# A decoder layer on one core: a piece behind the weighting in four quads, and two pieces of the row maximum copied by ScalarE and merged by GpSimd

## The chip, the cores and the metric

One core of one Trainium2 chip runs the whole kernel in one launch. The metric is the device time in microseconds; lower is better. TensorE does the matmuls, VectorE (DVE) and ScalarE (ACT) read what it leaves in PSUM, GpSimd (POOL) works on SBUF, SyncE (SP) issues most transfers.

## The reference, cut to what matters

The layer is causal self-attention, then attention over a context, then a mixture of experts, each followed by a layer norm. The change is in the self-attention, with S = 2048 rows, D = 256, H = 16 heads of 16 columns:

```python
scores = jnp.einsum('bhqd,bhkd->bhqk', q, k) / jnp.sqrt(jnp.float32(Dh))
causal = jnp.tril(jnp.ones((S, S), dtype=bool))
scores = jnp.where(causal[None, None], scores, jnp.float32(-jnp.inf))
attn = jax.nn.softmax(scores, axis=-1)
out = jnp.einsum('bhqk,bhkd->bhqd', attn, v)
```

The softmax is computed with the maximum of each row of scores taken off, and that maximum is found before the head's exponentials are.

## The kernel before

`project` forms q, k, v and the context's matrices, `attend` does the 16 heads, `finish` the rest. The change touches `attend`, and one place in `project`.

**A head** is cut into ten quads (QUADS), each of 512 queries by four tiles of 128 keys; quads 0, 2, 5 and 9 are on the diagonal and smaller. In each quad s, TensorE's queue holds in this order: the first half of the scores (`scores_half(h, s, 0)`, L747, two matmuls, one in each half of the array's rows, the row groups 0 and 1; on the diagonal also the small matmuls of L756 that hide later keys), the entries of place 0, the second half of the scores, the entries of place 1, the weighing of the quad two before (`weigh`, L774, fp32, eight matmul records, all 128 rows), and the entries of place 2. `scores_half` of the next quad waits until ScalarE has taken the exponential of the same half (L709, 1024 or 640 columns, written to `probs`). ScalarE also copies the accumulator `acc` when a block of queries ends (L714, behind the exponentials of quads 1, 2, 4 and 7), and the folded sums (L721, quad 4). A block's first weighing waits for the copy of the block before.

**The maximum of the rows** is found a head or two ahead. For it the scores are formed once more with queries on the partitions, in 35 pieces of up to 512 columns (`form_piece`, L154, and L161 for the diagonal), each in a bank of a ring of three (`ring`, NRING = 3). A piece uses one row group: `given` adds up the columns that each group has had since the last half of scores, and the group with the smaller sum takes the next piece (the first on a tie). Its VectorE reduction (`reduce_piece`, L172) writes a column or more of `partial` and frees the bank; TensorE waits for the bank's last user before it forms entry e + 3. Three other entries run through the ring: "F" folds the sums of the head before (copied by ScalarE), "M" turns `neg_max`, and "T" turns the folded sums, which VectorE normalises (L836, L838).

The table PLACES says which entries stand in the three places of each quad: "w" a whole piece of 512, "d" one on the diagonal, "n" one of 384, "p" and "q" two of 256 and four of 128 together. The pieces of quads 0 to 5 are for the next head, those of quads 6 to 9 (EARLY_QUADS) for the one after it. So the last piece for the next head stands in quad 5; behind it VectorE reduces `partial` to `neg_max` (L850) and waits for that before it goes on, since `partial` is written again. In quad 8 the maximum goes through the ring, VectorE writes `max_row` (L855), and SyncE sends it to the rows of `qstack` that the next head's scores wait for. The first head's pieces, and the early ones of the second, are formed in `project` (`pieces_behind`), 51 in all.

**GpSimd** meanwhile turns the experts' weights to two f16 halves, a sixteenth a head: multiply (L684), cast (L687), subtract (L689), each on 2304 columns. SyncE loads and stores them at the head's end, behind the maximum's rows and the loads of a later head's stacks.

Of the kernel before, what the change touches and what calls it, by code (L numbers as in the profile page):

```python
# [8 lines left out]
H = 16  # L9
# [4 lines left out]
P = 128  # L14
# [40 lines left out]
def cut_pieces():  # L55
# [11 lines left out]
    for quarters, found in share.items():  # L67
# [26 lines left out]
(FOLD_AT,) = [s for s, places in enumerate(PLACES) if "F" in "".join(places)]  # L94


def kind_of(n):
    if len(PIECES[n]) > 1:
        return {2: "p", 4: "q"}[len(PIECES[n])]
    ((t, c, w),) = PIECES[n]  # L100
    return "n" if w < QB else "d" if c + w == (t + 1) * P else "w"
# [16 lines left out]
def ring_of(h):  # L118

    def entry(s, x):  # L120
        kind, ahead = OTHERS[x] if x in OTHERS else ("piece", 2 if s in EARLY_QUADS else 1)
        return (kind, h + ahead, 0 if x in OTHERS else x)
# [8 lines left out]
TAKEN = [sum(x[0] != "fold" for x in ENTRIES[0:e + 1]) for e in range(len(ENTRIES))]  # L131
FOLDS = [sum(x[0] == "fold" for x in ENTRIES[0:e + 1]) for e in range(len(ENTRIES))]
# [33 lines left out]
def reduce_piece(nc, X, ALU, bank, partial, n):  # L166

    found = partial[:].rearrange("p t b -> p (t b)")
# [31 lines left out]
def decoder_layer(nc, x, xT, ctx_n, ctxT, wq, wk, wv, wo, b_qk, bv, bo, lm, w_all, gT, out):  # L200
# [15 lines left out]
    with whole:  # L216
# [10 lines left out]
        with ExitStack() as two:  # L227
            attn = two.enter_context(nc.sbuf_tensor("attn", [P, NT, DH + D], f32))
            with ExitStack() as three:
# [6 lines left out]
                partial = three.enter_context(nc.sbuf_tensor("partial", [P, NT, NQ], f32))  # L236
# [22 lines left out]
def project(nc, f32, f16, ALU, ACT, x, xT, ctx_n, ctxT, wq, wk, wv, wo, b_qk, bv, bo, lm, gT,  # L259
# [7 lines left out]
    with es:  # L267
# [183 lines left out]
        def _(dve):  # L451
# [7 lines left out]
            def take_pieces(count):  # L459
                nonlocal taken  # L460
                for _ in range(count):
# [4 lines left out]
                    if m == NPIECE:  # L466
                        dve.wait_ge(first_max_found, 1)
                    reduce_piece(nc, X, ALU, piece_ps[m % NRING], partial, FIRST_PIECES[m]).then_inc(piece_done, 1)
                    taken += 1
                    if taken == NPIECE:  # L470
                        dve.wait_ge(piece_done, NPIECE)
                        nc.vector.tensor_reduce(out=neg_max[:], in_=partial[:], axis=X, op=ALU.max, negate=True).then_inc(first_max_found, 1)
# [108 lines left out]
def attend(nc, f32, f16, bf16, ALU, ACT, X, q_split, k_split, w_all, w_split_d, res, bo_rows, ident32, attn, values,  # L581
# [6 lines left out]
    with es:  # L588
# [8 lines left out]
        folded = sb("folded", [P, QB], f32)  # L597
        inv = sb("inv", [P, 2, TPQ, NQ, 1], f32)
# [7 lines left out]
        ring_ready, ring_done, fold_copied = sem("ring_ready"), sem("ring_done"), sem("fold_copied")  # L606
        max_found = sem("max_found")
# [6 lines left out]
        def wait_taken(engine, e):  # L614

            if ENTRIES[e][0] == "fold":
                engine.wait_ge(fold_copied, FOLDS[e])
# [31 lines left out]

        block = es.enter_context(nc.Block())  # L650
# [1170 lines left out]
```

## Time and profile before

| | us |
|---|---|
| median of 3 runs | 841.28 |
| lowest and highest | 839.92, 846.05 |
| the profiled execution | 842.19 |
| its span, from the first to the last instruction | 840.5 |
| mean granted TensorE clock | 0.981 |

A span is what the traced instructions cover; an execution's time holds a little more. Times in the rows below are microseconds from the span's start. The `attend` part runs from 88.3 to about 470 us.

### The profile page before, as it was taken

How to read it: one execution, taken by the hardware profiler on the slowest of the kernel's cores; microseconds unless marked ns; L12 is line 12 of the kernel's file. 1: busy time of each engine (PE TensorE's matmuls, PEld its weight loads, DVE VectorE, ACT ScalarE, POOL GpSimd, SP SyncE). 2: the span in 40 equal slices, each digit the busy share in tenths (PEclk: the TensorE clock that was granted, in tenths of full speed). 3: DMA queues.
4: the chain of work that ended last, by engine and by line, in shares of the span. 5: the costliest groups of instructions: out<-in, count | busy, mean ns of one | idle time of the engine just before them, and what ended most of it. 6: DMA issues, size and time to landing. Idle time of an engine off the chain costs nothing. (4 is left out here: it accounts for less than half of the span.)

```text
span 840.5 us, 19596 instructions
## 1 busy us (share of the span) xinstructions
PE 788.1 (94%) x7434; PEld 494.6 (59%) x7435; DVE 555.8 (66%) x1072; ACT 513.0 (61%) x756; POOL 304.3 (36%) x226
## 2 busy tenths in 40 slices
PE   5899999999999999999998798889999999999994
PEld 1367334434444434444433586778888888877883
DVE  4575699999999999999980397973333333322395
ACT  4441587778877877788879487354444444343543
POOL 5040595554333455553640012142333333301121
PEclk9999799999999999999999998999999999999997
DMA  9683343333444433334332498462222222221362
GB/s 299 124 215 152 113 150 104 101 127 133 146 151 152 152 118 108 113 132 138 113 115 114 191 411 202 147 209 60 76 76 75 75 76 75 78 59 51 98 198 76
DMA packets 68362, 111.47 MB, mean 133 GB/s; under 512 B 39485, under 2 KB 49918, under 8 KB 63934
## 3 DMA queue, kind: packets, MB, share of 16 engines
q1 hardware_dynamic: 63134, 93.36, 35.4%
q0 software_dynamic: 4816, 16.65, 6.0%
q10 hardware_dynamic: 336, 0.40, 0.4%
q8 instruction: 54, 0.88, 0.4%
q14 instruction: 22, 0.18, 0.1%
HBM read 66.60 MB, written 32.37 MB: 118 GB/s over the span
## 5 line engine op out<-in xcount | busy, mean ns | idle before, releaser
L172 DVE TENSOR_REDUCE partial<-ring 128x1 f32<-128x512 f32 (+3 forms) x509 | 308.6, 667 | 28.4 <-PE ring L154 18.4
L709 ACT ACTIVATE probs<-scores 128x1024 f32<-128x1024 f32 (+1 forms) x320 | 271.5, 902 | 65.5 <-PE scores L756 31.8
L1284 ACT ACTIVATE hid<-turned 128x512 f32<-128x512 f32 (+1 forms) x112 | 65.6, 586 | 160.6 <-PE turned L1445 130.6
L774 PE MATMUL acc<-probs,values 128*32 128x512 f32 (+2 forms) x1472 | 156.4, 495 | 0.5 <-ACT acc_sb L714 0.3
L1470 PE MATMUL ops<-weights,work 128*128 (+1 forms) x1320 | 148.9, 273 | 2.6 <-issue 2.0
L154 PE MATMUL ring<-kstack,qstack 48*128 48x512 f16 (+1 forms) x580 | 147.8, 354 | 2.5 <-DVE partial L172 0.2
L1445 PE MATMUL turned<-mats,weights 128*128 128x256 f16 (+1 forms) x1344 | 144.2, 262 | 2.4 <-DMA mats<-attn 1.6
L1470 PEld LDWEIGHTS ops<-weights,work 128*128 128x128 f16 x1320 | 128.4, 98 | 18.8 <-issue 3.8
L1685 DVE TENSOR_TENSOR work<-hid,work 128x512 f16<-128x512 f32 (+1 forms) x112 | 76.8, 690 | 94.8 <-ACT work L1289 94.8
L684 POOL TENSOR_TENSOR a_w_in<-a_w_in,w_scale 128x2304 f32<-128x2304 f32 x16 | 64.4, 4026 | 204.2 <-DMA a_w_in<-w_all 204.2
L1445 PEld LDWEIGHTS turned<-mats,weights 128*128 (+1 forms) x1344 | 122.5, 98 | 21.0 <-issue 3.7
L747 PE MATMUL scores<-qstack,kstack 49*128 49x512 f16 (+3 forms) x640 | 127.8, 353 | 4.5 <-ACT probs L709 3.2
L1209 POOL DMA_INDIRECT by_token<-attn,dest_u x39 | 38.7, 992 | 143.5 <-DVE attn L1694 137.7
L154 PEld LDWEIGHTS ring<-kstack,qstack 48*128 48x128 f16 x580 | 44.3, 94 | 77.5 <-DVE partial L172 63.4
L747 PEld LDWEIGHTS scores<-qstack,kstack 49*128 49x128 f16 x640 | 39.0, 94 | 80.6 <-ACT probs L709 58.0
L689 POOL TENSOR_TENSOR a_w_out<-a_w_in,a_w_out 128x2304 f16<-128x2304 f32 x16 | 73.1, 4569 | 1.3
L1289 ACT ACTIVATE work<-hid 128x512 f16<-128x512 f32 (+1 forms) x112 | 69.7, 622 | 4.6
L774 PEld LDWEIGHTS acc<-probs,values 128*32 128x32 f32 x1472 | 43.5, 108 | 36.6 <-issue 25.6
L1694 DVE COPY attn<-ops 128x512 f32<-128x512 f32 (+1 forms) x20 | 13.6, 678 | 68.7 <-PE ops L1470 68.7
L161 PE MATMUL ring<-hide_keys,ident 64*128 64x128 bf16 x460 | 51.3, 203 | 0.0
L161 PEld LDWEIGHTS ring<-hide_keys,ident 64*128 64x128 bf16 x460 | 41.3, 95 | 15.6 <-issue 0.7
L1201 POOL DMA_INDIRECT attn<-rows_d,token_u x39 | 38.5, 988 | 30.0 <-issue 10.7
(203 smaller groups left out, 741.0 us busy)
## 6 DMA issues: line engine op xcount, KB each, us to landing
a_w_in<-w_all SPq DMA_DIRECT2D x16, 1152.0 KB, 8.9
w_split_d<-a_w_out SPq DMA_DIRECT2D x16, 1152.0 KB, 5.6
weights<-w_split_d SPq DMA_DIRECT2D x6, 2048.0 KB, 19.8
weights<-w_split_d POOLq DMA_DIRECT2D x3, 2048.0 KB, 11.8
qstack<-q_split SPq DMA_DIRECT2D x72, 64.0 KB, 2.7
kstack<-k_split SPq DMA_DIRECT2D x72, 64.0 KB, 2.7
weights<-by_token SPq DMA_DIRECT2D x8, 512.0 KB, 7.6
attn<-xT SPq DMA_DIRECT2D x4, 512.0 KB, 7.5
```

The source lines that it names most:

```text
L154: mm = nc.tensor.matmul(bank[:, at:at + w], qstack[rows, slot, t * P:(t + 1) * P], kstack[rows, slot, c:c + w], start=True, stop=not diagonal)
L161: mm = nc.tensor.matmul(bank[:, at - P + a:at - P + b], ident16[rows, copy], hide_keys[rows, copy, a:b], start=False, stop=part == 1)
L172: return nc.vector.tensor_reduce(out=found[:, places[0]:places[-1] + 1:step], in_=bank[:, 0:WIDTH[n]].rearrange("p (k w) -> p k w", k=len( ...
L689: nc.gpsimd.tensor_tensor(w_out[:, h % 2, 1], w_in[:, h % 2], w_out[:, h % 2, 0], ALU.subtract).then_inc(w_lo, 1)
L709: nc.scalar.activation(probs[:, quad % NPROBS, at:at + w], scores[half][:, first:first + w], ACT.Exp, scale=QK_SCALE).then_inc(exp_done, 1)
L747: mm = nc.tensor.matmul(scores[half][:, at:at + w], kstack[used, slot, kt * P:(kt + 1) * P], qstack[used, slot, (qb + 1) * QB - w:(qb + 1) ...
L774: mm = nc.tensor.matmul(acc[VW * group:VW * (group + 1), first_query:first_query + w], values[:, h, k0 + j], probs[:, quad % NPROBS, at:at ...
L1284: nc.scalar.activation(h32, hps[b].rearrange("p (j n) -> p j n", n=TW)[:, :, 0:w], ACT.Silu, scale=1.0 / WSCALE).then_inc(silu_done, 1)
L1289: nc.scalar.activation(hid[:, parity, 0, b * HB:(b + 1) * HB, 0:w], h32, ACT.Copy).then_inc(hid_hi, 1)
L1445: mm = nc.tensor.matmul(place.rearrange("p (g n) -> p g n", n=P), weights[:, a, bass.ds(at + (k * HID + (b * HB + j) * P), P)], turned_row ...
L1470: mm = nc.tensor.matmul(bank[:, i], hid[:, parity, a, j, i * P:(i + 1) * P], weights[:, c, bass.ds(at + (WE // 2 + j * D), D)], start=(m = ...
L1685: nc.vector.tensor_tensor(hid[:, parity, 1, chunks, 0:w], hid32[:, b % 2].rearrange("p (j n) -> p j n", n=TW)[:, :, 0:w], hid[:, parity, 0 ...
```

## The change

- PLACES: in quads 0, 2, 5 and 6 one "w" now stands in place 2, behind the weighing; it comes out of place 0 of the quad after (quads 1, 3, 6, 7). One "w" of quad 0 and one of quad 2 become "c".
- The two "c" are the first two column blocks of the last row tile (t = 15). TensorE forms them as before. Then ScalarE copies the bank to `copies` in SBUF (behind the exponentials of quads 0 and 2) and frees the bank; VectorE doesn't reduce them.
- GpSimd merges the two copies by a maximum, written as a + clamp(b - a), in twelve dependent operations: three on 512 columns, then three on each of 256, 128 and 64, which fold the halves of the copy onto one another. It does so between the cast and the subtraction of the weights.
- VectorE takes the maximum of what is left (64 columns to 2) and then reduces `partial` to `neg_max`; both stand ahead of the last entry of quad 7 (MAX_BEHIND), no longer behind the last piece in quad 5. It waits for GpSimd there.
- `partial` has two sets, one for even and one for odd heads.
- In `project` 50 pieces are formed and not 51, since the early quads hold one fewer.

```diff
-PLACES = (("", "wd", ""), ("ww", "w", "nw"), ("", "ww", ""), ("dw", "w", "w"), ("", "ww", "Fwp"),
-          ("", "wn", ""), ("ww", "d", ""), ("ww", "n", "w"), ("qMT", "wd", "nw"), ("", "ww", "wp"))
+PLACES = (("", "cd", "w"), ("w", "w", "nw"), ("", "cw", "w"), ("d", "w", "w"), ("", "ww", "Fwp"),
+          ("", "wn", "w"), ("w", "d", "w"), ("w", "n", "w"), ("qMT", "wd", "nw"), ("", "ww", "wp"))
...
+MAX_BEHIND = 7
+MERGED = 64
...
-        return 2 if n % 4 == 3 else 1 if n == DC * CT - 1 else 0
+        return 2 if n % 4 == 3 else 0
...
-                partial = three.enter_context(nc.sbuf_tensor("partial", [P, NT, NQ], f32))
+                partial = three.enter_context(nc.sbuf_tensor("partial", [P, 2, NT, NQ], f32))
...
+            def merge_copies(g):
+
+                at = (g - 1) * MERGES
+                pool.wait_ge(ring_copied, COPIES[COPIED[g][-1]])
+                w = QB
+                while w >= MERGED:
+                    a, b = (copies[:, 0], copies[:, 1]) if w == QB else (copies[:, 0, 0:w], copies[:, 0, w:2 * w])
+                    if w < QB:
+                        pool.wait_ge(merged, at)
+                    nc.gpsimd.tensor_tensor(above[:, 0:w], b, a, ALU.subtract).then_inc(merged, 1)
+                    pool.wait_ge(merged, at + 1)
+                    nc.gpsimd.tensor_scalar(above[:, 0:w], above[:, 0:w], -NEG, 0.0, ALU.min, ALU.max).then_inc(merged, 1)
+                    pool.wait_ge(merged, at + 2)
+                    nc.gpsimd.tensor_tensor(a, a, above[:, 0:w], ALU.add).then_inc(merged, 1)
+                    at += 3
+                    w //= 2
...
+            def copy_piece(g, i):
+                e = COPIED[g][i]
+                act.wait_ge(ring_ready, e + 1)
+                if i == 0 and g > 1:
+                    act.wait_ge(merged_found, g - 1)
+                nc.scalar.activation(copies[:, i], ring[e % NRING][:], ACT.Copy).then_inc(ring_copied, 1)
...
                     exps(h, s)
+                    if s in COPY_AT and h + 1 < H:
+                        copy_piece(h + 1, COPY_AT.index(s))
...
+                if e in MAX_FOUND_AT:
+                    found = MAX_FOUND_AT[e]
+                    dve.wait_ge(ring_done, TAKEN[LAST_PIECE[found]])
+                    dve.wait_ge(merged, found * MERGES)
+                    nc.vector.tensor_reduce(out=partial[:, found % 2, NT - 1, 0:2], in_=copies[:, 0, 0:MERGED].rearrange("p (k w) -> p k w", k=2),
+                                            axis=X, op=ALU.max).then_inc(merged_found, 1)
+                    dve.wait_ge(merged_found, found)
+                    nc.vector.tensor_reduce(out=neg_max[:], in_=partial[:, found % 2], axis=X, op=ALU.max,
+                                            negate=True).then_inc(max_found, 1)
                 dve.wait_ge(ring_ready, e + 1)
                 if kind == "piece":
-                    reduce_piece(nc, X, ALU, bank, partial, n).then_inc(ring_done, 1)
-                    if e == LAST_PIECE[g]:
-                        dve.wait_ge(ring_done, TAKEN[e])
-                        nc.vector.tensor_reduce(out=neg_max[:], in_=partial[:], axis=X, op=ALU.max,
-                                                negate=True).then_inc(max_found, 1)
-                        dve.wait_ge(max_found, g)
+                    reduce_piece(nc, X, ALU, bank, partial, g, n).then_inc(ring_done, 1)
```

## Rows read from the trace of the kernel before

**Rows 1.** The page, part 1: engine, busy us (share of the span), instructions.
```profile
PE 788.1 (94%) x7434; PEld 494.6 (59%) x7435; DVE 555.8 (66%) x1072; ACT 513.0 (61%) x756; POOL 304.3 (36%) x226
```

**Rows 2.** Busy time in a 25 us stretch of attention; then clock, DMA share, GB/s.
```profile
core 0: us, PE busy (x) PEld busy (x) DVE busy (x) ACT busy (x) POOL busy (x), PEclk, DMA share, GB/s
225.00:250.00 25.00, 24.74 (x264) 10.06 (x262) 23.31 (x42) 20.20 (x27) 11.52 (x4) 1.00 0.38 128
```

**Rows 3.** VectorE's timeline over one head: start, length, instruction, idle before it.
```profile
205.52 0.27 DVE L855 TENSOR_SCALAR max_row<-ring 16x128 f16<-16x128 f32 x1
...
212.88 4.14 DVE L172 TENSOR_REDUCE partial<-ring 128x1 f32<-128x512 f32 x7 [0.31 <-PE ring L154]
217.31 3.84 DVE L172 TENSOR_REDUCE partial<-ring 128x1 f32<-128x512 f32 x6 [0.30 <-PE ring L161]
221.73 2.35 DVE L172 TENSOR_REDUCE partial<-ring 128x1 f32<-128x512 f32 x4 [0.57 <-PE ring L154]
224.11 0.22 DVE L850 TENSOR_REDUCE neg_max<-partial 128x16 f32<-128x64 f32 x1
224.54 4.94 DVE L172 TENSOR_REDUCE partial<-ring 128x1 f32<-128x512 f32 x8 [0.20 <-PE ring L154]
229.39 0.27 DVE L855 TENSOR_SCALAR max_row<-ring 16x128 f16<-16x128 f32 x1
```

**Rows 4.** VectorE's timeline from 226.5 us on.
```profile
226.52 2.95 DVE L172 TENSOR_REDUCE partial<-ring 128x1 f32<-128x512 f32 x5
```

**Rows 5.** TensorE's timeline from 223.8 to 225 us: quad 6.
```profile
223.83 0.39 PE L747 MATMUL scores<-qstack,kstack 49*128 49x512 f16 x2
224.05 0.38 PE L154 MATMUL ring<-kstack,qstack 48*128 48x512 f16 x2
...
224.88 0.64 PE L774 MATMUL acc<-probs,values 128*32 128x512 f32 x4
```

**Rows 6.** TensorE's weight loads over the same head, with what they waited for.
```profile
215.28 0.09 PEld L154 LDWEIGHTS ring<-kstack,qstack 48*128 48x128 f16 x1 [0.32 <-DVE partial L172]
...
219.22 0.10 PEld L747 LDWEIGHTS scores<-qstack,kstack 49*128 49x128 f16 x2 [0.47 <-ACT probs L709]
...
222.25 0.31 PEld L154 LDWEIGHTS ring<-kstack,qstack 48*128 48x128 f16 x2 [0.15 <-ACT folded L721]
...
222.83 0.16 PEld L774 LDWEIGHTS acc<-probs,values 128*32 128x32 f32 x8
```

**Rows 7.** TensorE's timeline from 217.5 to 219.6 us: a lone piece behind a weighing.
```profile
217.64 1.06 PE L774 MATMUL acc<-probs,values 128*32 128x512 f32 x8
218.64 0.39 PE L154 MATMUL ring<-kstack,qstack 48*128 48x512 f16 x1
218.65 0.97 PE L747 MATMUL scores<-qstack,kstack 49*128 49x512 f16 x4
```

**Rows 8.** Groups by line and shape, 130 to 400 us: busy, mean ns, idle before.
```profile
L172 DVE TENSOR_REDUCE partial<-ring 128x1 f32<-128x512 f32 x317 | 202.4, 683 | 17.3 <-PE ring L154 11.9 <-PE ring L161 3.3
```

**Rows 9.** ScalarE's timeline over the same head.
```profile
212.69 1.94 ACT L709 ACTIVATE probs<-scores 128x1024 f32<-128x1024 f32 x2 [0.79 <-PE scores L747]
...
214.99 1.32 ACT L709 ACTIVATE probs<-scores 128x640 f32<-128x640 f32 x2
216.74 0.60 ACT L714 ACTIVATE acc_sb<-acc 128x512 f32<-128x512 f32 x1 [0.43 <-PE acc L774]
217.24 3.99 ACT L709 ACTIVATE probs<-scores 128x1024 f32<-128x1024 f32 x4
```

**Rows 10.** GpSimd's timeline over the same head.
```profile
223.32 4.03 POOL L684 TENSOR_TENSOR a_w_in<-a_w_in,w_scale 128x2304 f32<-128x2304 f32 x1 [12.81 <-DMA a_w_in<-w_all]
227.41 2.10 POOL L687 CAST a_w_out<-a_w_in 128x2304 f16<-128x2304 f32 x1
229.59 4.57 POOL L689 TENSOR_TENSOR a_w_out<-a_w_in,a_w_out 128x2304 f16<-128x2304 f32 x1
```

**Rows 11.** GpSimd's groups by line and shape: its shortest rows with two large inputs.
```profile
L443 POOL TENSOR_TENSOR values<-values,bv_rows 128x256 f32<-128x256 f32 x16 | 11.2, 721 | 29.4 <-ACT values L387 29.4
```

**Rows 12.** GpSimd's timeline in the first head.
```profile
97.94 2.10 POOL L687 CAST a_w_out<-a_w_in 128x2304 f16<-128x2304 f32 x1
```

More of the change, by code:

```diff
@@ L87 @@
 EARLY_QUADS = tuple(range(6, NQUAD))
[L91 to L92 removed]
+PLACES = (("", "cd", "w"), ("w", "w", "nw"), ("", "cw", "w"), ("d", "w", "w"), ("", "ww", "Fwp"),
+          ("", "wn", "w"), ("w", "d", "w"), ("w", "n", "w"), ("qMT", "wd", "nw"), ("", "ww", "wp"))
 OTHERS = {"M": ("max", 1), "F": ("fold", -1), "T": ("turn", -1)}
 (FOLD_AT,) = [s for s, places in enumerate(PLACES) if "F" in "".join(places)]
+COPY_AT = [s for s, places in enumerate(PLACES) if "c" in "".join(places)]
+MAX_BEHIND = 7
+MERGED = 64
+assert len(COPY_AT) == 2
 def kind_of(n):
@@ L100, in kind_of @@
     ((t, c, w),) = PIECES[n]
+    if t == NT - 1 and c // QB < len(COPY_AT):
+        return "c"
     return "n" if w < QB else "d" if c + w == (t + 1) * P else "w"
@@ L120, in entry @@
     def entry(s, x):
-        kind, ahead = OTHERS[x] if x in OTHERS else ("piece", 2 if s in EARLY_QUADS else 1)
+        kind, ahead = OTHERS[x] if x in OTHERS else ("copied" if kind_of(x) == "c" else "piece", 2 if s in EARLY_QUADS else 1)
         return (kind, h + ahead, 0 if x in OTHERS else x)
@@ L130 @@
 ENTRY_AT = {x: e for e, x in enumerate(ENTRIES)}
-TAKEN = [sum(x[0] != "fold" for x in ENTRIES[0:e + 1]) for e in range(len(ENTRIES))]
-FOLDS = [sum(x[0] == "fold" for x in ENTRIES[0:e + 1]) for e in range(len(ENTRIES))]
+BY_ACT = ("fold", "copied")
+TAKEN = [sum(x[0] not in BY_ACT for x in ENTRIES[0:e + 1]) for e in range(len(ENTRIES))]
+COPIES = [sum(x[0] in BY_ACT for x in ENTRIES[0:e + 1]) for e in range(len(ENTRIES))]
+COPIED = {g: [e for e, (kind, of, _) in enumerate(ENTRIES) if (kind, of) == ("copied", g)] for g in range(1, H)}
+MAX_FOUND_AT = {ENTRY_AT[([x for place in RING[g - 1][MAX_BEHIND] for x in place] or [("max", g, 0)])[-1]]: g for g in range(1, H)}
 LAST_PIECE = {g: e for e, (kind, g, _) in enumerate(ENTRIES) if kind == "piece"}
@@ L163, in form_piece, with reduce_piece @@
     return mm
-def reduce_piece(nc, X, ALU, bank, partial, n):
-    found = partial[:].rearrange("p t b -> p (t b)")
+def reduce_piece(nc, X, ALU, bank, partial, g, n):
+    found = partial[:, g % 2].rearrange("p t b -> p (t b)")
     places = [t * NQ + c // QB for t, c, _ in PIECES[n]]
@@ L471, in take_pieces @@
                         dve.wait_ge(piece_done, NPIECE)
-                        nc.vector.tensor_reduce(out=neg_max[:], in_=partial[:], axis=X, op=ALU.max, negate=True).then_inc(first_max_found, 1)
+                        nc.vector.tensor_reduce(out=neg_max[:], in_=partial[:, 0], axis=X, op=ALU.max, negate=True).then_inc(first_max_found, 1)
                     if taken == NPIECE + 2:
@@ L597, in attend @@
         folded = sb("folded", [P, QB], f32)
+        copies = sb("copies", [P, 2, QB], f32)
+        above = sb("above", [P, QB], f32)
         inv = sb("inv", [P, 2, TPQ, NQ, 1], f32)
@@ L720, in copy_folded @@
                     act.wait_ge(ring_ready, ENTRY_AT["turn", h - 1, 0] + 1)
-                nc.scalar.activation(folded[:], ring[e % NRING][:], ACT.Copy).then_inc(fold_copied, 1)
+                nc.scalar.activation(folded[:], ring[e % NRING][:], ACT.Copy).then_inc(ring_copied, 1)
+            def copy_piece(g, i):
[4 more added lines that the diff above has]
+                nc.scalar.activation(copies[:, i], ring[e % NRING][:], ACT.Copy).then_inc(ring_copied, 1)
             for h in range(H):
@@ L800, in through_ring @@
                         wait_taken(pe, e - NRING)
-                    if kind == "piece":
+                    if kind in ("piece", "copied"):
                         group = given.index(min(given))
```

19 lines of the change are left out of this document (10 added, 9 removed).

## The prediction

> **What bounds the kernel now.** The page comes first: TensorE is busy 94% of the span, VectorE 66%, and both are crowded only while attention runs [rows 1]. The table by stretches shows that part alone: in 25 us of attention TensorE is busy 24.74, VectorE 23.31, ScalarE 20.20 and GpSimd 11.52 us [rows 2]. So three engines are near their limits, and the share of busy time can't say which one sets the pace. What does is the order within one head. A head lasts 229.39 - 205.52 = 23.87 us (from one writing of max_row to the next, [rows 3]), and the head I walk through is that one. It has ten quads. In each, TensorE writes scores, forms pieces into the ring of three banks, and weighs (the fp32 matmuls of L774).
>
> The VectorE timeline [rows 3] shows idle time before four groups of reductions (0.31 us at 212.88, 0.30 at 217.31, 0.57 at 221.73, 0.20 at 224.54), each time until TensorE had formed a piece. From 226.52 on there is none up to the maximum at 229.39: five reductions in 2.95 us, then max_row [rows 3, 4]. So VectorE sets the pace only in the last third of the head (quads 7 to 9, and on into quad 0 of the next); in quads 0 to 6 it waits for TensorE. There TensorE runs without a hole: after the weighing at 222.83 scores start at 223.83, two pieces side by side at 224.05, and the next weighing at 224.88, 2.05 us in all [rows 5]. The waits of TensorE's loads in the same head [rows 6] are for VectorE at 215.28, for ScalarE at 219.22 and 222.25. (An idle of weight loads behind a weighing is mostly its own streaming, 1.00 us from 217.64 to 218.64 [rows 7], and is no wait.)
>
> **The change, part by part.**
>
> *Two pieces a head off VectorE.* A reduction of 512 costs 0.68 us alone [rows 8] and about 0.60 from start to start (five in 2.95 us, one of them a shorter one [rows 4]). Two fewer are 1.2 us a head less. But they leave in quads 0 and 2, just ahead of the idle at 212.88 and 217.31 [rows 3], where the next piece isn't formed yet: the saved time becomes longer idle. One small thing is gained: the wait at 215.28 for a bank gets shorter by up to 0.2. I count the removal as 0. The other bound is the whole 1.2 us (the first rival).
>
> *One piece behind the weighting in quads 0, 2, 5 and 6.* Before, quads 1, 3, 6 and 7 form two pieces side by side ahead of the second scores. Now one stands directly behind the weighing, the other alone. This needn't cost TensorE anything. At 218.64 a lone piece (row group 1) starts with the scores of row group 0 (218.65), and the second scores matmul follows in the group that comes free [rows 7]. The next lone piece then goes to group 0 beside it. Reading `given`: in quads 0, 2 and 6 the smaller sum is that of group 1, so the piece pairs so. In quad 5 it is a tie (384 + 384 against 256 + 512), and the index of the minimum is group 0. Then group 0 has one stream of 512 more, and that costs what one takes, 224.05 - 223.83 = 0.22 us [rows 5]. The gain: VectorE gets its first piece behind a weighing 0.22 us sooner. The loss: the second scores matmul comes 0.22 later, and the exponential behind it 0.18 (estimate: it takes the start of the last matmul).
>
> *ScalarE's two copies.* Nearest row: the 512 copy from PSUM, 0.60 us, 0.50 from its start to the next exponential (216.74 to 217.24) [rows 9]. The first copy falls into ScalarE's idle before 212.69, which it fits. The second: ScalarE works without a break from 212.69 to 216.31 and has 0.43 us idle before 216.74 [rows 9]. All this now comes 0.18 later, the copy ends near 216.94 and the accumulator's copy starts near 216.82. That is 0.08 late. But the piece of quad 3 (formed at about 216.8 now) needs the bank that the copy frees at 216.99: TensorE stands 0.18 us, with the second scores and the weighing of quad 3 queued behind it. Of that 0.10 is returned at 219.22, where TensorE waited for an exponential anyway [rows 6], and 0.08 stays. The wait for `folded` at 222.25 doesn't add to it, since the diagonal piece next to it waits for VectorE as long. With the tie's 0.22 TensorE is 0.28 us late (0.07 + 0.21 before rounding) at the weighing in quad 7. Bounds: 0 (all waits swallow it) to 0.45 (the `folded` path passes on its 0.18).
>
> *VectorE's maximum, now at the end of quad 7.* Before, one reduction of 64 columns at 224.11, 0.22 us, half in an idle stretch [rows 3]. After, two in a chain, the second of which waits for the first, ahead of the last piece of quad 7, in the stretch without idle: 0.22 + 0.03 + 0.22, less 0.05 that the next overlaps, 0.42 us. The 0.03 is what lies between the four reductions that ended at 221.73 + 2.35 = 224.08 and the one at 224.11 that waited for them [rows 3]. Bounds 0.35 and 0.60. The maximum's transpose and everything behind it on VectorE wait for that.
>
> *GpSimd's merging.* Twelve dependent operations a head on 512, 256, 128 and 64 columns. Nearest rows: 2304 columns with two inputs 4.03 us (1.75 ns a column), with one input 2.10 (0.91); 256 columns 0.72 us (2.8 ns) [rows 10, 11]. The two-input ones, 2 x 960 columns, give 3.4 us at 1.75 and 5.4 at 2.8, the others 0.9 to 2.7, twelve hand-overs of some 0.07 (227.35 to 227.41 [rows 10]) 0.9 us: 5.2 to 9.0, I take 7.3. The second copy ends at 216.9 and VectorE asks for the result near 228.2 (226.52 + 2.95, less the last two reductions, 1.28 [rows 4]), so 11.3 us hide it. GpSimd has room: 10.8 of 23.87 us busy a head. The store and the next load of the weights queue behind its last subtraction, which ends about 216.9 + 7.3 + 4.6 = 228.8, before SyncE comes to it at the head's end. In the first head merging can begin only when the cast ends, 97.94 + 2.10 = 100.04 [rows 12], later in the head's course than in any other; what its cover lacks there is lost once and not in every head.
> The Trainium skill (GPSIMD Engine Reference, "Elementwise — side-by-side cycle accounting") gives 4497 ns for a two-input operation on 2048 columns, 2.2 ns a column. By it the two-input ones would take 4.2 us instead of 3.4 at the long rows' rate, and the sum for the head would be unchanged. The page's larger price isn't what this case's 4.03 us for 2304 columns shows.
>
> *Partial maxima in two sets.* They drop a wait of VectorE that [rows 3] shows at 224.33 to 224.54, in idle time: 0. One piece fewer in the projection takes one reduction, 0.68 us [rows 8], off its end and adds as much to the first head.
>
> **The sum.** At the end of quad 7 VectorE is late by 0.28 (TensorE's delay) - 0.22 (the piece behind the weighing) + 0.42 (the two reductions) = 0.48 us. From there to quad 0 of the next head the two are bound to each other, so the head is 0.48 longer. There are 13 full heads (the first starts loosely; the last two form few pieces or none ahead): 13 x 0.48 = 6.2 us. The profiled execution took 842.19 us, 840.5 of it the span; 840.5 + 6.2 = 846.7, and 842.19 + 6.2 = 848.4. It lies 0.9 above the median of the runs, 841.28, so the median should be 841.28 + 6.2 = 847.5.
>
> **The rivals.**
> A. VectorE is the bound throughout. For it: 23.31 of 25 us busy. Then the head shortens by 1.2 - 0.42 = 0.78 us, over 14 heads 10.9: 830.4. Against it: four idles a head, two of them where the pieces are taken off. It decides if those idles disappear.
> B. The delays are swallowed: TensorE 0 late, and 0.42 - 0.22 = 0.20, with the bank's wait at 215.28 gained back: 0 to 0.2 a head, 841 to 844; I say 842. For it: three waits of TensorE a head that may give way.
> C. All delays add: 0.45 - 0.22 + 0.60 = 0.83 a head, 13 x 0.83 = 10.8: 852.
> D. Merging is too long. At over 11.3 us VectorE stands in front of it in every head; at 13 us that is 1.7 us x 15 = 25: 867. Against it: even the rate of the shortest row gives 9.0.
>
> **How the numbers follow.** My forecast 0.50 (843.5 to 851 by itself), A 0.09, B 0.20, C 0.15, D 0.06. What a measurement of this kernel can tell from no change is about 1%, 8.4 us: below 832.9, above 849.7. Faster: A, 0.08. Slower: C, D and three tenths of the forecast, 0.35. Within: 0.57. The range leaves out A, D and edges: 838 to 855, which reaches from B to C.
>
> **What would show it.** In the profile after: a head of about 24.35 us; VectorE idle before the first piece of quads 1 and 3 longer than 0.3 us; ScalarE's copies near 0.6 us; TensorE waiting for ScalarE's second copy for some 0.2 us; the weighings around the tie 0.2 further apart; both small reductions near 0.22 us in a stretch without idle; GpSimd's twelve operations done in 5 to 9 us before VectorE asks. I am wrong if the idles behind the weighings vanish (A), if no weighing comes later than before up to quad 7 (B), or if VectorE waits for GpSimd (D).

## The result and the profile after

| | before | after |
|---|---|---|
| median, us (lowest to highest) | 841.24 (839.92 to 846.05) | 849.91 (846.77 to 850.99) |
| the profiled execution, its span | 842.19, 840.5 | 850.39, 848.6 |
| mean granted TensorE clock | 0.981 | 0.978 |
| one head, max_row to max_row | 23.87 | 24.39 |

The changed kernel takes 1.0089 times the time before, with an interval from 1.0070 to 1.0109. The span is 8.1 us longer, and 8.0 of it lies ahead of the end of attention: from the span's start to the first matmul behind attention it is 472.24 us before and 480.25 after. The page, part 1, of the kernel after (engine, busy us, share, instructions), and the same 25 us of attention as in [rows 2]:

```profile
PE 790.6 (93%) x7434; PEld 499.3 (59%) x7435; DVE 544.5 (64%) x1057; ACT 526.5 (62%) x786; POOL 409.1 (48%) x406
```
```profile
225.00:250.00 25.00, 24.19 (x266) 10.43 (x260) 22.01 (x40) 20.56 (x29) 18.26 (x16) 1.00 0.40 128
```

VectorE fell from 23.31 to 22.01 us busy in the stretch and TensorE from 24.74 to 24.19, at a granted clock of 1.00 (2.4 GHz) in both. TensorE has the same work in each head, but a head takes longer, so that less of it falls into 25 us. More is waited for. One head on VectorE after, to be held against [rows 3] (start, length, instruction, idle before it and what ended it):

```profile
257.27 0.27 DVE L900 TENSOR_SCALAR max_row<-ring 16x128 f16<-16x128 f32 x1
...
264.41 3.58 DVE L182 TENSOR_REDUCE partial<-ring 128x1 f32<-128x512 f32 x6 [0.62 <-PE ring L164]
268.61 1.98 DVE L182 TENSOR_REDUCE partial<-ring 128x1 f32<-128x512 f32 x3 [0.62 <-PE ring L164]
271.05 1.99 DVE L182 TENSOR_REDUCE partial<-ring 128x1 f32<-128x512 f32 x3 [0.46 <-PE ring L164]
273.62 2.35 DVE L182 TENSOR_REDUCE partial<-ring 128x1 f32<-128x512 f32 x4 [0.57 <-PE ring L164]
276.14 1.89 DVE L182 TENSOR_REDUCE partial<-ring 128x1 f32<-128x512 f32 x3 [0.17 <-PE ring L164]
278.41 1.75 DVE L182 TENSOR_REDUCE partial<-ring 128x1 f32<-128x512 f32 x3 [0.39 <-PE ring L164]
280.08 0.21 DVE L890 TENSOR_REDUCE partial<-copies 128x2 f32<-128x64 f32 x1
280.33 0.22 DVE L893 TENSOR_REDUCE neg_max<-partial 128x16 f32<-128x64 f32 x1
280.46 1.28 DVE L182 TENSOR_REDUCE partial<-ring 128x1 f32<-128x512 f32 x2
281.66 0.27 DVE L900 TENSOR_SCALAR max_row<-ring 16x128 f16<-16x128 f32 x1
```

The idles that ended four groups before (0.31, 0.30, 0.57, 0.20) are now six (0.62, 0.62, 0.46, 0.57, 0.17, 0.39): 1.38 us before and 2.83 after in all. The time of the two reductions taken away became idle time. The two small reductions stand with no idle around them, 280.46 - 280.08 = 0.38 us from the first to the piece behind.

The head on TensorE, by its weight loads: the L815 rows are the weighings (of quads 1, 2, 3, 5 and 6 here), and the two others each follow a wait.

```profile
264.96 0.58 PEld L815 LDWEIGHTS acc<-probs,values 128*32 128x32 f32 x12 [0.43 <-issue]
...
267.21 0.28 PEld L815 LDWEIGHTS acc<-probs,values 128*32 128x32 f32 x8
...
268.79 0.09 PEld L164 LDWEIGHTS ring<-kstack,qstack 48*128 48x128 f16 x1 [0.50 <-ACT copies L760]
...
269.63 0.16 PEld L815 LDWEIGHTS acc<-probs,values 128*32 128x32 f32 x8 [0.43 <-issue]
...
271.11 0.10 PEld L788 LDWEIGHTS scores<-qstack,kstack 49*128 49x128 f16 x2 [0.37 <-ACT probs L741]
...
274.71 0.16 PEld L815 LDWEIGHTS acc<-probs,values 128*32 128x32 f32 x8
...
276.99 0.16 PEld L815 LDWEIGHTS acc<-probs,values 128*32 128x32 f32 x8
```

From such starts a table can be made: column s is the time from the weighing in quad s to that in quad s + 1, and column 9 goes on to quad 0 of the next head (267.21 - 264.96 = 2.25 is column 1; the weighing of quad 4, at 271.65, is left out of the fence). The columns add up to the head, to 0.01 us. The experiments are read in the same way, so these four rows stand here for all (e2 and e3 are described below):

| kernel | 0 | 1 | 2 | 3 | 4 | 5 | 6 | 7 | 8 | 9 | head |
|---|---|---|---|---|---|---|---|---|---|---|---|
| before | 1.97 | 2.40 | 2.04 | 2.12 | 3.07 | 2.06 | 2.00 | 3.26 | 2.39 | 2.57 | 23.87 |
| after | 1.97 | 2.25 | 2.42 | 2.02 | 3.06 | 2.28 | 2.01 | 3.42 | 2.39 | 2.57 | 24.39 |
| e2, placement alone | 1.97 | 2.25 | 2.04 | 2.11 | 3.06 | 2.28 | 2.01 | 3.07 | 2.39 | 2.57 | 23.75 |
| e3, copies alone | 1.97 | 2.40 | 2.04 | 2.12 | 3.07 | 2.06 | 2.00 | 3.64 | 2.39 | 2.57 | 24.25 |

So +0.52 a head comes from four places: -0.16 in column 1, +0.29 in columns 2 and 3 together, +0.22 in column 5 and +0.16 in column 7. Over 13 heads that is 6.8 us. The other 1.2 are single events: 0.3 at the first maximum (110.26 before, 110.54 after), 0.3 in the last head that still finds a maximum for the next, and 0.6 in the third. The third head on VectorE and on GpSimd:

```profile
158.12 0.22 DVE L890 TENSOR_REDUCE partial<-copies 128x2 f32<-128x64 f32 x1 [0.50 <-POOL copies L706]
```
```profile
134.45 9.32 POOL L726 TENSOR_TENSOR res<-res,bo_rows 128x1024 f32<-128x1024 f32 x4
...
150.00 1.27 POOL L702 TENSOR_TENSOR above<-copies 128x512 f32<-128x512 f32 x1
...
157.70 0.32 POOL L706 TENSOR_TENSOR copies<-copies,above 128x64 f32<-128x64 f32 x1
```

The bias additions, once in the kernel, take 9.32 us on GpSimd and push the third head's merging so late that VectorE stands 0.50 us for it.

### The profile page after: what moved, and what is told of

It is laid out like the page before. It is cut to its first block and busy times, and to the rows that moved or that the text cites. A ratio compares the mean times of both kernels' runs of the same rounds, so it can differ in the third digit from the quotient of the medians.

```text
span 848.6 us, 19820 instructions
## 1 busy us (share of the span) xinstructions
PE 790.6 (93%) x7434; PEld 499.3 (59%) x7435; DVE 544.5 (64%) x1057; ACT 526.5 (62%) x786; POOL 409.1 (48%) x406
## 5 line engine op out<-in xcount | busy, mean ns | idle before, releaser
L182 DVE TENSOR_REDUCE partial<-ring 128x1 f32<-128x512 f32 (+3 forms) x480 | 296.9, 669 | 48.7 <-PE ring L164 44.9
L164 PE MATMUL ring<-kstack,qstack 48*128 48x512 f16 (+1 forms) x581 | 157.8, 354 | 4.4 <-ACT copies L760 0.7
L815 PE MATMUL acc<-probs,values 128*32 128x512 f32 (+2 forms) x1472 | 156.4, 495 | 0.5 <-ACT acc_sb L746 0.3
L788 PE MATMUL scores<-qstack,kstack 49*128 49x512 f16 (+3 forms) x640 | 139.5, 353 | 7.1 <-ACT probs L741 5.9
L164 PEld LDWEIGHTS ring<-kstack,qstack 48*128 48x128 f16 x581 | 47.3, 94 | 126.1 <-DVE partial L182 100.3
L702 POOL TENSOR_TENSOR above<-copies 128x512 f32<-128x512 f32 (+3 forms) x60 | 41.7, 694 | 72.9 <-ACT copies L760 69.2
L815 PEld LDWEIGHTS acc<-probs,values 128*32 128x32 f32 x1472 | 43.5, 109 | 36.7 <-issue 26.6
```

The source lines that it names most:

```text
L164: mm = nc.tensor.matmul(bank[:, at:at + w], qstack[rows, slot, t * P:(t + 1) * P], kstack[rows, slot, c:c + w], start=True, stop=not diagonal)
L182: return nc.vector.tensor_reduce(out=found[:, places[0]:places[-1] + 1:step], in_=bank[:, 0:WIDTH[n]].rearrange("p (k w) -> p k w", k=len( ...
L788: mm = nc.tensor.matmul(scores[half][:, at:at + w], kstack[used, slot, kt * P:(kt + 1) * P], qstack[used, slot, (qb + 1) * QB - w:(qb + 1) ...
L815: mm = nc.tensor.matmul(acc[VW * group:VW * (group + 1), first_query:first_query + w], values[:, h, k0 + j], probs[:, quad % NPROBS, at:at ...
```

## The experiments

All are timed beside the kernel before on the same chip. "Head" is from max_row to max_row in the trace; it is that of a head in the middle of attention, and from the fifth head on all full heads of a trace agree to 0.02 us. It leaves out the first heads and their single events, which differ between executions (last section), so it is the finer measure of what the change does in each head. The times of several of these kernels can't be told apart by their intervals, only by their heads.

| run | median us | ratio to before (interval) | head us |
|---|---|---|---|
| e1_tie | 847.90 | 1.0082 (1.0054 to 1.0110) | 24.14 |
| e2_places_only | 839.84 | 0.9976 (0.9962 to 0.9989) | 23.75 |
| e3_copies_only | 846.87 | 1.0061 (1.0035 to 1.0086) | 24.25 |
| e4_max6_bias_last | 847.61 | 1.0057 (1.0037 to 1.0076) | 24.04 |
| e5_places_tie | 839.11 | 0.9969 (0.9953 to 0.9985) | 23.64 |
| e6_c2_second | 850.01 | 1.0107 (1.0085 to 1.0129) | 24.39 |
| e7_late_copies | 842.26 | 1.0002 (0.9985 to 1.0018) | 23.87 |
| e8_late_places | 839.74 | 0.9979 (0.9961 to 0.9998) | 23.63 |
| e9_three_places | 836.25 | 0.9935 (0.9915 to 0.9955) | 23.53 |
| e10_short_n | 837.18 | 0.9943 (0.9923 to 0.9962) | 23.61 |
| e11_short_copy | 845.35 | 1.0046 (1.0026 to 1.0067) | 24.10 |
| e12_round_trip | 835.05 | 0.9937 (0.9921 to 0.9953) | 23.55 |

**The change taken apart.** First the tie of the row groups in quad 5, undone by the order of its two pieces (against after):

```diff
-          ("", "wn", "w"), ("w", "d", "w"), ("w", "n", "w"), ...
+          ("", "nw", "w"), ("w", "d", "w"), ("w", "n", "w"), ...
```


> The changed kernel with the two pieces of quad 5 in the other order (n, w), so that there is no tie and the piece behind the weighing goes to row group 1. My theory (TensorE's delay up to quad 7 sets the extra time): weighings around it 2.06 us apart instead of 2.28, the head 24.39 - 0.22 = 24.17 us, the kernel 3 us faster than the changed one, 847 us (3 over 13 heads' 0.22). Rival (the tie costs nothing, the delay is ScalarE's and VectorE's alone): head 24.39 us, 850 us.

The head fell by 0.25. Column 5 went from 2.28 to 2.06, as the theory says. Column 6 rose by 0.14 (a wait for an exponential that had been covered) and column 7 fell by as much; the remaining 0.03 is in column 4. The time alone doesn't show the gain: the interval of e1's ratio holds that of the changed kernel. Its profile has larger single events than the changed kernel's. VectorE stands 0.99 us for GpSimd in the third head, which takes 25.23 us, and the one behind it takes 25.53: there the granted clock is 0.50 (1.2 GHz) from 158.2 to 161.5 us, directly behind that wait, and 1.00 on both sides of it.

Then the placement alone (before, with the new places and "w" for "c"; 50 pieces in the projection), and the copies alone (after, with the old places):

```diff
-PLACES = (("", "cd", "w"), ("w", "w", "nw"), ("", "cw", "w"), ("d", "w", "w"), ...
+PLACES = (("", "wd", "w"), ("w", "w", "nw"), ("", "ww", "w"), ("d", "w", "w"), ...
```


> The kernel before with the pieces placed as in the changed one, all reduced by VectorE, the maximum where its last piece is (now place 2 of quad 5); no copies, no merging, one set of partial maxima. My theory: the tie's +0.22 and the lone reduction of the maximum behind the piece, against 0.22 gained by the earlier piece: head 23.87 + 0.1 us, 841.5 to 844, I say 842.5. Rival (VectorE is the bound, and the earlier pieces fill its idle time): 0.3 us a head less, 837.

```diff
-PLACES = (("", "cd", "w"), ("w", "w", "nw"), ("", "cw", "w"), ("d", "w", "w"), ...
+PLACES = (("", "cd", ""), ("ww", "w", "nw"), ("", "cw", ""), ("dw", "w", "w"), ...
```


> The changed kernel with the pieces placed as before the change; ScalarE still copies the two, GpSimd merges, and both small reductions stand at the end of quad 7. My theory: the two reductions cost 0.38 us a head in VectorE's stretch without idle time and nothing else does: head 24.25 us, plus once 0.6 us for GpSimd in the third head: 841.2 + 5.5 = 846.7. Rival (VectorE is the bound throughout): 0.8 us a head less than before, 830.

e3 came out as expected: with the old placement only column 7 differs from before, by 0.38, which is the small reductions; copies and merging cost nothing in a head in the middle of attention. ScalarE's timeline shows where the second copy went, first in e3, then what e2 has at the same place (no copy):

```profile
217.63 0.65 ACT L760 ACTIVATE copies<-ring 128x512 f32<-128x512 f32 x1
218.22 0.60 ACT L746 ACTIVATE acc_sb<-acc 128x512 f32<-128x512 f32 x1
```
```profile
212.40 1.32 ACT L709 ACTIVATE probs<-scores 128x640 f32<-128x640 f32 x2
213.81 0.60 ACT L714 ACTIVATE acc_sb<-acc 128x512 f32<-128x512 f32 x1
```

In e3 the copy stands in the idle of 0.43 us ahead of the accumulator's copy [rows 9]. It begins 0.16 us ahead of the end of the exponential before it and occupies ScalarE for 0.48 (worked out below), so it needs 0.32 of that idle, and the accumulator's copy starts 3.54 us behind the weighing of quad 1, as it does before. In e2 the idle is only 213.81 - 212.40 - 1.32 = 0.09 us: the new placement has used it up, and with it a copy makes ScalarE 0.23 late. e2 was a miss of 0.2 a head (23.97 was expected): the placement makes the head shorter by 0.12, even with the tie's 0.22 in it, since columns 1 and 7 gain 0.16 and 0.19. The parts are not independent: 23.75 + 0.38 = 24.13, and after takes 24.39.

The small reductions, moved from quad 7 to the end of quad 6, where VectorE has an idle, and the bias additions to the last head:

```diff
-MAX_BEHIND = 7
+MAX_BEHIND = 6
...
-                if h == 1:
+                if h == H - 1:
```


> The changed kernel with the two small reductions ahead of the last piece of quad 6 instead of quad 7 (VectorE is idle there for 0.39 us), and GpSimd's four additions of the output bias behind the last head instead of the second, so that merging is not late. My theory: the reductions cost nothing there, head 24.39 - 0.38 = 24.01 us; 0.6 us of the third head saved, up to 1 us lost in the first, where merging ends late: 841.2 + 2 to 3.5 = 844. Rival (what costs is only TensorE's and ScalarE's delay, the reductions are free at either place): head 24.39, 849.

The head is 24.04, shorter than after by 0.35, and column 7 is back at 3.07. So the price of the small reductions was that of the place, not of the work. In the first head the sooner place has a price of its own. VectorE's timeline of e4 there, and then a stretch of it (last columns: granted clock, DMA share, GB/s):

```profile
107.56 0.22 DVE L890 TENSOR_REDUCE partial<-copies 128x2 f32<-128x64 f32 x1 [3.18 <-POOL copies L706]
```
```profile
109.00:112.00 3.00, 3.00 (x22) 1.52 (x19) 2.33 (x6) 1.57 (x2) 3.00 (x2) 0.50 0.00 0
```

VectorE stands 3.18 us for the merging, TensorE has nothing to do for 2.59 us of it, and from 108.9 to 115.8 us the granted clock is at its lower level (1.2 GHz). The interval from the first maximum to the second takes 25.62 us for it, though the merging is in time there. So less than 13 x 0.35 shows in the median.

**What the second copy costs.** If the wait for the bank at 268.79 is the cause, it should help to let TensorE come to that bank later:

```diff
-PLACES = (("", "cd", "w"), ("w", "w", "nw"), ("", "cw", "w"), ...
+PLACES = (("", "cd", "w"), ("w", "w", "nw"), ("", "wc", "w"), ...
```


> The changed kernel with the copied piece of quad 2 formed second and not first (w, c), so that its bank is needed by the second piece of quad 3 and no longer by the diagonal one. If TensorE's wait for that bank is what makes the stretch of quads 1 to 4 0.14 us longer than before, it goes away: head 24.25, 848. If it is ScalarE's queue (the copy's own length ahead of the accumulator's copy and of the exponentials of quad 3), the wait for the bank goes and comes back as a wait for an exponential: the weighing of quad 3 comes 0.17 us sooner and that of quad 4 less than 0.05, head 24.35 us, 849.5. I expect the second.

The wait for the bank is gone and nothing is gained: column 2 went from 2.42 to 2.13 and column 3 from 2.02 to 2.31. TensorE's weight loads in e6, the row that answers to after's 271.11 with its 0.37:

```profile
269.20 0.10 PEld L788 LDWEIGHTS scores<-qstack,kstack 49*128 49x128 f16 x2 [0.63 <-ACT probs L741]
```

So it is ScalarE's queue that is late, and the bank was only where it was seen first. A copy cut from 512 to 64 columns (from the second head on; the other columns of the second copy aren't taken into the maximum) tells the size:

```diff
+                width = MERGED if i == 1 and g > 1 else QB
-                nc.scalar.activation(copies[:, i], ring[e % NRING][:], ACT.Copy)
+                nc.scalar.activation(copies[:, i, 0:width], ring[e % NRING][:, 0:width], ACT.Copy)
```


> The changed kernel with the copy of quad 2 taken over 64 of its 512 columns (from the second head on; the rest of that piece is left out of the maximum), some 0.37 us less for ScalarE. If ScalarE's queue is what the copies cost in quads 1 to 4 (0.29 us against the same placement without copies), the weighing of quad 4 comes 0.25 to 0.29 sooner and the head takes 24.39 - 0.27 = 24.1 us, 846. If it isn't (something else of the copies, GpSimd's reads for one), 24.39 and 850.

The head fell by 0.29 (column 2 to 2.05, column 3 to 2.11), all that e2 and after differ by in these columns. ScalarE's timeline, first of after, then of e11:

```profile
266.45 0.60 ACT L746 ACTIVATE acc_sb<-acc 128x512 f32<-128x512 f32 x1
266.93 1.32 ACT L741 ACTIVATE probs<-scores 128x640 f32<-128x640 f32 x2
268.09 0.65 ACT L760 ACTIVATE copies<-ring 128x512 f32<-128x512 f32 x1
268.57 0.66 ACT L746 ACTIVATE acc_sb<-acc 128x512 f32<-128x512 f32 x1
269.05 2.02 ACT L741 ACTIVATE probs<-scores 128x1024 f32<-128x1024 f32 x2
```
```profile
266.89 0.27 ACT L761 ACTIVATE copies<-ring 128x64 f32<-128x64 f32 x1
267.14 0.60 ACT L746 ACTIVATE acc_sb<-acc 128x512 f32<-128x512 f32 x1
```

There is no idle left around the copy; it occupies ScalarE for 268.57 - 268.09 = 0.48 us, and 267.14 - 266.89 = 0.25 when short. That is 0.23 less, and the head fell by 0.29: the two exponentials behind it also take 2.02 us in after, against 1.94 of such a pair in [rows 9], and why they are longer there is open. With that, the two costs add up: 24.39 - 0.35 (e4) - 0.29 (e11) = 23.75, the head of e2.

**Is VectorE the bound in quads 7 to 9?** The prediction said so. Then copies there must pay, where two reductions go from the stretch without idle. e7 is after with the old placement, the "c" in quads 8 and 9 (two heads ahead), the small reductions ahead of quad 6's first entry and the bias additions last:

```diff
+          ("", "wn", ""), ("ww", "d", ""), ("ww", "n", "w"), ("qMT", "dc", "nw"), ("", "wc", "wp"))
-MAX_BEHIND = 7
+MAX_BEHIND = 6
```


> The placement of the kernel before; the two copied pieces moved from quads 0 and 2 to quads 8 and 9 (for the head after the next), where VectorE has no idle time; GpSimd merges them in the next head, the two small reductions stand ahead of the first piece of quad 6, where VectorE is idle, and the bias additions behind the last head. My theory (a reduction taken off VectorE is worth something only where TensorE waits for it): the waits of 0.26 and 0.21 us in quads 8 and 9 go, head 23.87 - 0.47 = 23.40 us, 841.2 - 6.5 = 834.7. Rival 1 (VectorE's load is no bound anywhere, TensorE's and ScalarE's order is): 23.87, 841. Rival 2 (VectorE's load is the bound wherever it is taken off): 23.87 - 0.78 = 23.1, 830, but then the copies in quads 0 and 2 would have shown it.

The theory fell. It gave 23.40 and the head is 23.87, that of before to the hundredth. TensorE's waits for VectorE have not moved. First two rows of before, then of e7:

```profile
279.94 0.09 PEld L154 LDWEIGHTS ring<-kstack,qstack 48*128 48x128 f16 x1 [0.24 <-DVE partial L172]
...
282.43 0.09 PEld L154 LDWEIGHTS ring<-kstack,qstack 48*128 48x128 f16 x1 [0.19 <-DVE partial L172]
```
```profile
280.82 0.09 PEld L164 LDWEIGHTS ring<-kstack,qstack 48*128 48x128 f16 x1 [0.24 <-DVE partial L182]
...
283.31 0.09 PEld L164 LDWEIGHTS ring<-kstack,qstack 48*128 48x128 f16 x1 [0.19 <-DVE partial L182]
```

TensorE's matmuls of e7 (in the fence that comes first) and VectorE's timeline at the same places:

```profile
279.75 0.40 PE L164 MATMUL ring<-kstack,qstack 48*128 48x384 f16 x2
...
280.83 0.39 PE L164 MATMUL ring<-kstack,qstack 48*128 48x512 f16 x1
```

```profile
280.21 1.75 DVE L182 TENSOR_REDUCE partial<-ring 128x1 f32<-128x384 f32 x3 [0.66 <-PE ring L171]
282.57 0.69 DVE L182 TENSOR_REDUCE partial<-ring 128x1 f32<-128x512 f32 x1 [0.60 <-PE ring L164]
```

TensorE waits 0.24 us for VectorE at 280.82, and VectorE has stood idle for 0.66 us just ahead of the reduction that TensorE waits for. That is no engine with too much to do. It is one bank's round trip: the 384-column piece is formed behind the weighing at 279.75, VectorE starts on it 0.46 us later, and the bank goes to the third entry behind it at 280.83, 0.62 after that. In the kernel before the wait of 0.24 was the same. There VectorE's reductions stand in one merged row (ten in 6.18 us from 277.99), which hid this; taken alone, the one of 384 columns is

```profile
279.33 0.56 DVE L172 TENSOR_REDUCE partial<-ring 128x1 f32<-128x384 f32 x1
```

and that is again 0.46 us behind its matmul, at 278.87.

e10 tests that: before, with quad 8's 384-column piece reduced over 128 of its columns (the others of that piece aren't taken into the maximum), and nothing else changed:

```diff
+    width = P if n in DEALT[8][2] and WIDTH[n] == QB - P else WIDTH[n]
```


> The kernel before, with the reduction of the 384-column piece of quad 8 taken over 128 of its columns only (the rest of that piece is left out of the maximum), 0.27 us less work for VectorE. Theory 1 (TensorE's 0.26 us wait in quad 9 is the round trip of that one bank: formed behind the weighing, 0.42 us until it can be read, 0.55 reduced, 0.05 until it is free): the wait goes, head 23.87 - 0.26 = 23.61 us, 838. Theory 2 (VectorE's load, or the order on TensorE and ScalarE, sets the quads 8 and 9): as when 1.2 us were taken off elsewhere, 23.87, 841.5.

The head is 23.61, as the round trip says: column 8 went from 2.39 to 2.12. The one reduction fell from 548 to 291 ns, 0.26 us, and that gives 0.26 a head, while 1.2 us off two others in the same stretch (e7) gave nothing. VectorE's timeline of e10 has the idles of the kernel before still in it (0.57 at 264.83), and the shorter head:

```profile
248.88 0.27 DVE L856 TENSOR_SCALAR max_row<-ring 16x128 f16<-16x128 f32 x1
...
264.83 2.35 DVE L173 TENSOR_REDUCE partial<-ring 128x1 f32<-128x512 f32 x4 [0.57 <-PE ring L154]
...
272.49 0.27 DVE L856 TENSOR_SCALAR max_row<-ring 16x128 f16<-16x128 f32 x1
```

**Versions to beat both.** e5 is e2 with the tie undone, e8 is e5 with the late copies of e7.

```diff
-          ("", "wn", "w"), ...
+          ("", "nw", "w"), ...
```


> The kernel before with the pieces placed as in the changed one and no tie in quad 5 (n, w), all reduced by VectorE, no copies. My theory: the placement alone gave a head of 23.75 us with TensorE 0.06 late in quad 7; without the tie it is 0.2 us early there, and VectorE with it: 23.5 to 23.6 us a head, 841.2 - 4 = 837. Rival (VectorE is now the bound and keeps the 23.75): 839.5.

```diff
+          ("", "nw", "w"), ("w", "d", "w"), ("w", "n", "w"), ("qMT", "dc", "nw"), ("", "wc", "wp"))
```


> Both together: one piece behind the weighing in quads 0, 2, 5 and 6 without the tie, and the copied pieces in quads 8 and 9, the small reductions ahead of the last piece of quad 6. My theory: the two gains are in different stretches and add: 23.5 - 0.45 = 23.05 us a head, 841.2 - 11 = 830. Rival (TensorE or ScalarE becomes the bound before both are paid out): no better than the late copies alone, 23.4 us, 834.7.

Swapping the pieces gives back half of the tie's 0.22: in quad 6 a wait for an exponential comes (TensorE's loads in e5):

```profile
271.12 0.10 PEld L747 LDWEIGHTS scores<-qstack,kstack 49*128 49x128 f16 x2 [0.39 <-ACT probs L709]
```

e8 equals e5 (23.63 and 23.64 a head, where 23.05 was expected): the late copies add nothing, again. So quad 5 had better stay as it was. e9 is before, with the piece behind the weighing in quads 0, 2 and 6 alone:

```diff
-PLACES = (("", "wd", ""), ("ww", "w", "nw"), ("", "ww", ""), ("dw", "w", "w"), ("", "ww", "Fwp"),
-          ("", "wn", ""), ("ww", "d", ""), ("ww", "n", "w"), ("qMT", "wd", "nw"), ("", "ww", "wp"))
+PLACES = (("", "wd", "w"), ("w", "w", "nw"), ("", "ww", "w"), ("d", "w", "w"), ("", "ww", "Fwp"),
+          ("", "wn", ""), ("ww", "d", "w"), ("w", "n", "w"), ("qMT", "wd", "nw"), ("", "ww", "wp"))
```


> The kernel before with one piece behind the weighing in quads 0, 2 and 6 only (quad 5 stays as it was), no copies. My theory of where the placement pays: 0.15 us in quad 2 (a bank is free sooner) and 0.19 in quad 8 (VectorE is no longer late with the last piece of quad 7), and quad 5's gave nothing back for the 0.14 that a wait for an exponential cost: head 23.87 - 0.34 = 23.53 us, 841.5 - 4.6 = 837. Rival (quad 5's piece is what gives the 0.19): 23.7, 839.5.

Exactly as expected, 23.53 a head, 23.87 - 0.16 - 0.19 with the rest as before: 836.25 us. It is faster than both kernels, without copies, merging or a second set of maxima. e12 takes one "w" from behind quad 8's weighing to quad 3, to take away the round trip that e10 found:

```diff
-          ... ("d", "w", "w"), ... ("", "wn", ""), ... ("qMT", "wd", "nw"), ...
+          ... ("dw", "w", "w"), ... ("", "wn", ""), ... ("qMT", "wd", "n"), ...
```


> The three placements (quads 0, 2 and 6, no copies), and one more whole piece moved from place 2 of quad 8 to place 0 of quad 3, beside the diagonal piece there. The second piece of quad 9 then takes the bank of the diagonal piece of quad 8, formed ahead of the weighing, and not that of the one formed behind it. If the round trip of that bank is the wait, 0.26 us go and the moved piece costs TensorE nothing in quad 3, since it pairs: head 23.53 - 0.26 = 23.27 us, 842.3 - 8.5 = 834. Rival (VectorE's one more reduction in quad 3 is passed on, or TensorE doesn't pair): 23.5, 837.

Column 8 fell to 2.12, as it should. But column 2 rose from 2.04 to 2.47. The reason on TensorE's loads:

```profile
259.96 0.09 PEld L154 LDWEIGHTS ring<-kstack,qstack 48*128 48x128 f16 x1 [0.57 <-DVE partial L172]
```

In quad 3 one more piece finds all three banks taken and waits for a reduction. Column 3 is 0.14 shorter for it (1.97), which leaves the sum where it was. The head is 23.55 against e9's 23.53, and the ratios (0.9937, 0.9935) can't be told apart: the rival was right.

## Why the prediction was right, and where it wasn't

The forecast was 847.5 (838 to 855); the median is 849.91. The sign, the size and the sum's result of 0.48 a head hold: 0.52 was measured. Step by step:

- **Two pieces off VectorE: 0.** Held. Their time became idle [rows 3 against the fence above]. Rival A, that VectorE bounds the head, fell.
- **The tie in quad 5: 0.22.** Held to the hundredth (2.06 to 2.28), and e1 takes it away.
- **The piece behind the weighing: -0.22 at the end of quad 7.** It was -0.19 (e2).
- **Small reductions: 0.42.** In e3 they cost 0.38, in after 0.35 (3.42 against e2's 3.07).
- **TensorE 0.28 late at the weighing in quad 7.** It was 0.36, the sum of columns 0 to 6 before rounding. Two terms were off and mostly cancelled. That the sum came so near is luck. The second copy was put at 0.08 and cost 0.29, because the cover that I gave it, ScalarE's idle of 0.43 ahead of the accumulator's copy [rows 9], had shrunk to 0.09 (e2). And column 1 gained 0.16. I had allowed "up to 0.2" for a bank freed sooner and counted it at 0, and I had the reason wrong: I put it down to the reductions taken off, but with these alone the column stays at 2.40 (e3), and with the placement alone it is 2.25 (e2). I had taken the wait for the bank at 268.79 for the mechanism; e6 shows that it was ScalarE's queue. Against e2, column 2 is 0.38 longer and column 3 gives 0.09 back, where I had 0.18 and 0.10.
- **Merging hidden.** Held in size: in the head at 257 us it runs from 268.88 to 276.89, 8.0 us where I took 7.3 and bounded 9.0, and VectorE asks at 280.08. The Trainium skill (GPSIMD Engine Reference, "Elementwise — side-by-side cycle accounting") gives 4497 ns for two inputs of 2048 columns; at that rate, 2.2 ns a column, 512 columns would take 1.13 us as an estimate. The trace has 1.27, where the 1.75 ns of the long rows would give 0.90, so that for these short operations the page is nearer. I had named the first head as the one with least cover. In the changed kernel it was enough there (merged at 107.33, asked for at 108.96), and the late one was the third, behind the bias additions, 0.6 us once. But in e4, where VectorE asks a quad sooner, it was the first, with 3.18 us.
- **"VectorE sets the pace in quads 7 to 9".** This step was wrong, though the number came out. A stretch without idle in the row, with TensorE waiting for VectorE, looked like a full engine. e7, e8 and e10 show that TensorE waits there for one bank. What remains true is narrower: just ahead of quad 7's last piece, two serial reductions are passed on (e3), and one quad sooner they are not (e4). The reading went wrong on a merged row that showed no idle: the one reduction that TensorE waits for started as soon after its matmul as in e7, where VectorE stood idle ahead of it.
- **The single events** weren't in the sum: 1.2 us, half of the 2.4 by which the forecast was low. The other half is the 0.04 a head (0.5 us) and the spread of the runs.

As a whole: the change joins a placement that gains 0.12 a head (0.34 without the tie), and copies that cost 0.64 in this placement, 0.35 for two small reductions in a bad place and 0.29 on ScalarE. The part that was to take load off VectorE gave nothing anywhere that it was tried.

Open is why swapping the tie's pieces exposes an exponential in quad 6 (column 6 +0.14 in e1 and e5). With the old placement (e3) the second copy costs nothing because ScalarE's idle of 0.43 holds it. That idle falls to 0.09 with the new one; in the trace of e2 column 1 is 0.16 shorter and the exponentials of quad 2 start 0.18 later, which makes up the 0.34, but no run takes the two apart.

## What to carry to other kernels

When an engine waits for another that has no idle, it need not be the other's load: add up the buffer's own round trip (formed, readable, reduced, free), and if that already fills the time, less load elsewhere is worth nothing (1.2 us gave 0), while a shorter instruction on that buffer's chain is worth all of it (0.26 gave 0.26). An operation added in an idle of its engine is free only if the idle is still there once the rest of the change is in; put small serial operations where the engine stands idle anyway (0.35 a head in quad 7, none in quad 6), and look at the first pass too, where what they wait for may not be ready (3.18 us once in e4). A wait that disappears with no gain (e6) names the symptom: follow the queue behind it.

## What the runs showed of the hardware

**Matmuls of different row groups start out of their order in the program, as the trace records it.** TensorE's timeline of the kernel before, where the two hiding matmuls of L161 stand ahead of the scores of L747 in the queue:

```profile
216.81 0.38 PE L154 MATMUL ring<-kstack,qstack 48*128 48x512 f16 x2
217.03 0.22 PE L161 MATMUL ring<-hide_keys,ident 64*128 64x128 bf16 x1
217.04 0.38 PE L747 MATMUL scores<-qstack,kstack 49*128 49x512 f16 x1
217.09 0.19 PE L161 MATMUL ring<-hide_keys,ident 64*128 64x64 bf16 x1
217.12 0.38 PE L747 MATMUL scores<-qstack,kstack 49*128 49x512 f16 x1
```

A scores matmul starts at 217.04, before the second hiding one at 217.09, which stands ahead of it; the other scores matmul starts behind both. The program's row groups fit this (the hiding ones share a group with the later of the two scores matmuls), but the rows don't print the group. The same order of starts stands once in each of 15 heads.

**GpSimd's short operations.** Two inputs take 1.27, 0.73, 0.46 and 0.32 us for 512, 256, 128 and 64 columns, one input with a minimum and a maximum by constants 0.61, 0.40, 0.29 and 0.24. From 64 to 512 columns that is 2.1 and 0.8 ns a column on top of some 0.2 us each: for the 64-column ones more than half is fixed, so folding down to 64 by dependent operations is dear. GpSimd's work didn't slow VectorE: a 512 reduction takes 686 ns on average after and 683 before.

**The first head's clock differs between executions.** The same 25 us (last columns: granted clock, DMA share, GB/s) in the profiled executions of before and then of e2, which up to there differ by one piece:

```profile
85.00:110.00 25.00, 22.92 (x190) 9.15 (x189) 18.43 (x31) 17.25 (x22) 15.94 (x5) 0.80 0.26 95
```
```profile
85.00:110.00 25.00, 22.44 (x213) 9.72 (x212) 19.65 (x35) 18.69 (x23) 16.31 (x5) 0.93 0.26 96
```

A mean of 0.80 means that part of the stretch ran at 1.2 GHz and part at 2.4. The first maximum came at 110.26 and 107.95 us. Over all kernels here it lay between 107.1 and 111.2: 107.1 to 110.3 in the six without copies, 108.6 to 111.2 in the eight with them. With one trace of each kernel, what the copies add there can't be told from the clock; only in e4 is a part of it, the wait of 3.18 us, plainly the edit's. That the clock differs between executions of one kernel, and the span with it, the runs show: of the 29 of the kernel before that were timed beside e5 to e8, the eight with a mean clock of 0.979 had spans of 840.8 to 842.5 us, the three with 0.986 or 0.987 had 837.5 to 838.1.
